# Layer 1 pipeline of a fused two-layer decoder: another order of the slots on TensorE and ScalarE

## What is computed

```python
# Lightning attention, 16 heads of 32, one chunk of 128 tokens
v, q, k = x @ Wv, x @ Wq, x @ Wk ; q, k = rotary(q), rotary(k)
o = (decay_mask * (q @ k.T)) @ v                    # per head
x = layernorm(x + (o * rsqrt(mean(o**2) + 1e-5) * rms_w) @ Wo)
# cross attention with ctx as keys and values: 8 heads of 16 tokens each,
# the 512 features are the positions
qk = einsum('hdq,hdl->hql', x_heads, ctx_heads) / sqrt(16)      # 512 x 512 per head
p = softmax(qk, axis=-1)
ret = einsum('hql,hdl->hdq', p, ctx_heads)
x = layernorm(x + gamma * ret)
```

## Time and profile before

| | |
|---|---|
| median of 3 runs | 3030.43 us (3025.59 to 3036.5) |
| the profiled execution | 3040.62 us |
| its span, first to last instruction | 3038.8 us |
| layer 0 | 0 to about 1164 us |
| layer 1 | about 1164 to 2061 us |
| experts | from about 2064 us |
| PE busy over the span | 2715.9 us (89%) |
| DVE / ACT / POOL busy | 45% / 29% / 19% |
| mean granted TensorE clock | 0.948 of 2.4 GHz |

### The profile page before, as it was taken

The page is one execution under the profiler, slowest core; times in us unless marked ns, Lnnn a source line. Parts: engine busy times, 40 slices in busy tenths (PEclk is TensorE's granted clock), DMA queues, the critical chain, the costliest instruction groups (busy, mean ns, idle before and its releaser), DMA issues. The chain is left out here.

```text
span 3038.8 us, 33792 instructions
## 1 busy us (share of the span) xinstructions
PE 2715.9 (89%) x10930; PEld 1371.9 (45%) x10990; DVE 1377.1 (45%) x2541; ACT 887.1 (29%) x1932; POOL 591.6 (19%) x632
## 2 busy tenths in 40 slices
PE   7999999999999765788888888867989999999998
PEld 3544553555455342333333333315445656656543
DVE  3545645564466253556566656642312222222245
ACT  2334343333434331134344434451001111111101
POOL 2111101110110001322222222200541111111153
PEclk9999999999999877999999999996999999999999
DMA  5110212021102104424444434323013333333144
GB/s 183 56 70 28 82 44 109 30 84 70 56 28 70 42 1 135 77 59 88 90 90 92 95 87 93 81 62 156 1 65 121 124 124 123 125 121 124 62 137 150
DMA packets 110237, 261.01 MB, mean 86 GB/s; under 512 B 21955, under 2 KB 55619, under 8 KB 98211
## 3 DMA queue, kind: packets, MB, share of 16 engines
q1 hardware_dynamic: 95202, 220.27, 24.3%
q0 software_dynamic: 13648, 38.06, 4.2%
q10 hardware_dynamic: 1264, 1.10, 0.1%
HBM read 203.76 MB, written 55.22 MB: 85 GB/s over the span
## 5 line engine op out<-in xcount | busy, mean ns | idle before, releaser
L2388 PE MATMUL d_bank<-d_w,d_xcol 128*128 x1280 | 406.4, 460 | 0.0
L1663 ACT ACTIVATE c_probs<-c_exp 128x512 f32<-128x512 f32 x512 | 277.9, 596 | 395.8 <-PE c_exp L1826 298.1
L1951 DVE TENSOR_REDUCE c_mx<-c_pair 128x2 f32<-128x1024 f32 x256 | 304.9, 1217 | 177.5 <-PE c_pair L1812 176.9
L742 PE MATMUL a_bank<-a_xT,a_ring 128*128 128x512 f32 x640 | 286.8, 600 | 10.9 <-DMA a_ident<-in_ident 10.9
L507 POOL TENSOR_TENSOR a_ry<-a_rt 128x512 f32<-128x512 f32 x80 | 128.8, 1610 | 803.0 <-DVE a_rt L994 803.0
L2388 PEld LDWEIGHTS d_bank<-d_w,d_xcol 128*128 128x128 f32 x1280 | 231.4, 191 | 102.1 <-issue 1.0
L2395 PE MATMUL d_bank<-d_w,d_hid 128*128 (+1 forms) x486 | 221.9, 592 | 0.7 <-DVE d_hid L2589 0.7
L742 PE MATMUL a_bank<-a_wo,a_ot 128*128 128x512 f32 x512 | 222.4, 592 | 0.0
L742 PEld LDWEIGHTS a_bank<-a_xT,a_ring 128*128 128x128 f32 x640 | 120.6, 192 | 150.0 <-issue 137.0
L1826 PE MATMUL c_exp<-c_qs,c_ks 128*128 128x512 bf16 x453 | 152.0, 392 | 35.4 <-ACT c_probs L1663 21.1
L2329 PE MATMUL d_bank<-d_xT,d_ws 128*128 128x512 f32 (+1 forms) x384 | 169.1, 601 | 0.7 <-ACT d_yrow L2309 0.7
(11 more groups left out here) (306 smaller groups left out, 3775.2 us busy)
## 6 DMA issues: line engine op xcount, KB each, us to landing
d_w<-in_w SPq DMA_DIRECT2D x16, 1408.0 KB, 6.5
scratch_results<-d_yrow SPq DMA_DIRECT2D x81, 256.0 KB, 2.0
a_ring<-in_wq SPq DMA_DIRECT2D x16, 1024.0 KB, 4.9
a_wo<-in_wo SPq DMA_DIRECT2D x16, 1024.0 KB, 4.9
c_ks<-scratch_kpark SPq DMA_DIRECT2D x96, 128.0 KB, 4.3
c_qs<-scratch_qpark SPq DMA_DIRECT2D x96, 128.0 KB, 4.3
d_w<-in_w SPq DMA_DIRECT2D x16, 768.0 KB, 8.4
a_ring<-in_w SPq DMA_DIRECT2D x8, 1024.0 KB, 8.4
```

Source lines behind the costliest of these rows:

```text
L742: ins = pe.matmul(bank[:, :], lhs(c), rhs(c), start=(c == 0), stop=(c == n - 1))
L1663: act.activation(probs[:, (LC * CH * n + k) % RING, :], bank[:, :], ACT.Exp, scale=float(CD) ** -0.5).then_inc(exped.sem, 1)
L1951: dve.tensor_reduce(mx[:, n % 2, at0:at0 + 2], bank[:, :].rearrange("p (i n) -> p i n", i=2), AX.X, ALU.max).then_inc(maxed.sem, 1)
L2388: ins = pe.matmul(bank[:, 0:FI], xcol[:, v, k, :], w13[:, bass.ds(at, 1), which, k, :].rearrange("p a n -> p (a n)"), start=(k == 0), stop ...
```

## The change

- `values` moves from the odd slots to the even ones, one slot earlier for each group of four exponentials (`turn_of`).
- `turn_x` moves from slot 0 of the phase in which its sequence is `a1` to slot 14 of the phase before (`TURN_X = 14`, for the new stage `a0 = p + 4`), between `scores` and `attend`; `PHASES` starts at -4. Its order in the small bank changes accordingly, and ACT copies it out in slot 15.
- `MAX_SLOTS` is 11: the 16 first products lie in 11 slots, and `TURN_MAX` is slot 11. DVE's `finish` and second `normalise`, and ACT's second root, come one slot earlier.
- In a slot ACT first drains the small bank (square, xT, sums, rms, v, turned q and k) and then does the two exponentials; the two roots of the layer norms stay behind the exponentials.
- The bank of the sum of squares counts as drained after the first of the two ACT steps of `rms_of`, which reads it, not after the second.
- On SP two rows of x are loaded ahead of the weights; after that `load_x(p + 5)` stands at the very end of a phase, behind `store(done)`, and from `p = 1` on it waits until that store has landed (`load_x` waits on `stored`).

```diff
-        rms_ready, y_added = signal("rms_ready", 1), signal("y_added", 1)
+        rms_step, y_added = signal("rms_step", 2), signal("y_added", 1)
-        PHASES = range(-3, SEQS + 1)
+        PHASES = range(-4, SEQS + 1)
         def stages(p):
-            return seq_at(p), seq_at(p + 1), seq_at(p + 2), seq_at(p + 3), seq_at(p - 1)
-        MAX_SLOTS = 12
-        TURN_X, SQUARES, OUT, V, Q, K = 0, 1, 2, 4, 6, 8
-        TURN_Q, TURN_K, TURN_MAX, SCORES, ATTEND = 10, 11, 12, 13, 15
+            return seq_at(p), seq_at(p + 1), seq_at(p + 2), seq_at(p + 3), seq_at(p + 4), seq_at(p - 1)
+        MAX_SLOTS = 11
+        SQUARES, OUT, V, Q, K = 1, 2, 4, 6, 8
+        TURN_Q, TURN_K, TURN_MAX, SCORES, TURN_X, ATTEND = 10, 11, 11, 13, 14, 15
         def turn_of(p, i):
-            if i % 2 == 0:
+            if i % 2:
                 return None
-            n, m = (p, (i - 3) // 2) if i >= 3 else (p - 1, TURNS - 1)
+            n, m = (p, i // 2 - 1) if i else (p - 1, TURNS - 1)
...
-                "ss": lambda: at(rms_ready, 1),
+                "ss": lambda: at(rms_step, 1),
...
             load_x(0)
+            load_x(1)
...
-                if seq_at(p + 4) is not None:
-                    load_x(p + 4)
                 if p > -2 and seq_at(p + 3) is not None:
                     load_c(p + 3)
                     load_cT(p + 3)
...
                 if done is not None:
                     store(done)
+                if p > -4 and seq_at(p + 5) is not None:
+                    load_x(p + 5)
...
             for p in PHASES:                       # scalar
                 for i in range(SLOTS):
-                    if x2 is not None:
-                        exp_of(x2, 2 * i)
-                        exp_of(x2, 2 * i + 1)
-                    if a2 is not None and i == TURN_X:
+                    if a2 is not None and i == 0:
                         square(a2)
-                    if a1 is not None and i == TURN_X + 1:
-                        turn_in(a1)
+                    if a0 is not None and i == TURN_X + 1:
+                        turn_in(a0)
...
                         turn(a1, 1)
-                    if done is not None and i == TURN_MAX + 2:
+                    if x2 is not None:
+                        exp_of(x2, 2 * i)
+                        exp_of(x2, 2 * i + 1)
+                    if a2 is not None and i == OUT + 2:
+                        root(a2, 0)
+                    if done is not None and i == SCORES:
                         root(done, 1)
...
             for p in PHASES:                       # tensor
                     if a1 is not None:
-                        if i == TURN_X:
-                            turn_x(a1)
...
                             attend(a1)
+                    if a0 is not None and i == TURN_X:
+                        turn_x(a0)
```

More of the change, by code:

```diff
@@ L1413, in build_layer1 @@
         for p in PHASES:
-            x2, x1, a2, a1, done = stages(p)
+            x2, x1, a2, a1, a0, done = stages(p)
             for i in range(SLOTS):
@@ L1424, in build_layer1 @@
                 if a1 is not None:
-                    for kind, at in (("xt", TURN_X), ("v", V), ("q", Q), ("k", K), ("qt", TURN_Q), ("kt", TURN_K),
-                                     ("a", ATTEND)):
+                    for kind, at in (("v", V), ("q", Q), ("k", K), ("qt", TURN_Q), ("kt", TURN_K), ("a", ATTEND)):
                         step_order += [(kind, a1)] if i == at else []
                     pair_order += [("s", a1, u) for u in range(2) if i == SCORES]
+                if a0 is not None:
+                    step_order += [("xt", a0)] if i == TURN_X else []
                 if (p, i) == FIX_TURN:
@@ L1682, in rms_of @@
                 bank = steps.wait(act, 0, ("ss", n))
-                astep.did(act.activation(lnv[:, 2:3], bank[:, 0:1], ACT.Ln, bias=eps[:, 0:1], scale=1.0 / D))
-                astep.wait(act, 0)
-                act.activation(rms[:, :], lnv[:, 2:3], ACT.Exp, scale=-0.5).then_inc(rms_ready.sem, 1)
+                act.activation(lnv[:, 2:3], bank[:, 0:1], ACT.Ln, bias=eps[:, 0:1], scale=1.0 / D)\
+                   .then_inc(rms_step.sem, 1)
+                rms_step.wait(act, n, 1)
+                act.activation(rms[:, :], lnv[:, 2:3], ACT.Exp, scale=-0.5).then_inc(rms_step.sem, 1)
             def root(n, i):
@@ L1715, in _ @@
                         rms_of(a2)
-                    if a2 is not None and i == OUT + 2:
-                        root(a2, 0)
                     if a1 is not None and i == V + 2:
@@ L1919, in add_y @@
                 bank = steps.wait(dve, 0, ("y", n))
-                rms_ready.wait(dve, n, 1)
+                rms_step.wait(dve, n, 2)
                 dve.scalar_tensor_tensor(row, bank[:, :], rms[:, 0:1], row, ALU.mult, ALU.add).then_inc(y_added.sem, 1)
@@ L1998, in _ @@
                         invert(done)
-                    if done is not None and i == TURN_MAX + 1:
+                    if done is not None and i == SCORES - 1:
                         finish(done)
@@ L2002, in _ @@
                         mask(a1)
-                    if done is not None and i == TURN_MAX + 3:
+                    if done is not None and i == SCORES + 1:
                         normalise(done, 1)
```

## The result

| | before | after |
|---|---|---|
| median | 3031.62 us (4 runs, 3025.59 to 3036.5) | 2913.68 us (4 runs, 2911.68 to 2917.99) |
| ratio | | 0.9614, 95% interval 0.9592 to 0.9635 |
| profiled execution | 3040.62 us | 2915.41 us |

The change gains 117.9 us, 3.9%. The forecast was 88 and its range ended at 2925, so it was too low by 30 us and the time lies outside the range.

The account below looks back on a forecast made before the run. PE was taken as the bound, its waits adding to each phase: 50.8 to 44.2 us saves 6.6, times 13 = 86, plus 2 at start and end = 88, giving 2943 us; range 2925 to 2987 at 0.8.

Parts of the forecast that it names:

- So 49.45 - 5.95 - 0.74 = 42.8 us of a phase is work: Clean phase of 49.45 us on PE, less 5.95 printed and 0.74 hidden waits, leaves 42.8 the change neither adds nor removes.
- The prediction's list of waits: PE's nine waits per clean phase: Wo, q, k, turned q, turned k, three at second products, turn_x; sum 5.95 us.
- Waits to come: New or remaining PE waits per phase: turned k 0.30, pairs of slots 12 and 13 0.35 and 0.1, attend 0.51; sum 1.4.
- The clock: First half of the Wo product, slow in 8 of 13 phases: full clock should hold with less waiting; otherwise 14 us less gain.
- Fits by 1 to 2 us: SP's chain from inverse to maxima takes 18.7 us plus c's loads, with 21.9 available: cost 0, else up to 2 per phase.
- Start and end: Load of x costs 1 us, phase -2 gains 2, phase -1 about 1, phases 13 to 16 nothing: together 2 us gained.
- The rivals: Four other outcomes: clock keeps falling (2956, 0.19), transfers bound (2975, 0.13), waits traded (3007, 0.10), slower at low clock (3048, 0.05).
- That of the transfers: Chain from inverse to maxima takes 2 to 3 us more, so slot 0 waits for DMA every phase: 2975 us, chance 0.13.
- that of the clock: Clock goes on falling because the stretch of turnings, scores and attend stays: 2956 us, chance 0.19.

Follow-up runs that it names:

- The forced waits: Changed kernel with PE waiting, in slots 3, 5 and 7 ahead of the second half product, on the slot's second exponential: 2993.27 us, ratio 0.9728.

## Why the prediction was too low, by its own steps

**The step that failed** is "So 49.45 - 5.95 - 0.74 = 42.8 us of a phase is work". It takes the idle time printed ahead of an instruction for the price of the wait, and the printed waits for all of them. The phases as measured leave 42.44 - 0.85 = 41.6 us of work, 1.2 less. The stretch from the first Wo half to turned q shows the error, since it holds the same instructions in both kernels: eight halves, eight pairs of second products, 22 matmuls of first products, four groups of values. Before it takes 1578.17 - 1548.34 = 29.83 us, after 1518.41 - (1534.12 - 42.44) = 26.73. The difference is 3.10, but only 0.74 + 0.67 + 0.67 = 2.08 was printed as idle. The timeline of PE before, at v, q and k:

```profile
1554.77 0.60 PE L1812 MATMUL c_pair<-c_ks,c_qs 96*128 96x512 bf16 x2
1555.44 1.96 PE L1784 MATMUL c_step<-c_wv,c_xT 128*128 128x512 f32 x4
...
1561.44 1.03 PE L1812 MATMUL c_pair<-c_ks,c_qs 96*128 96x512 bf16 x4
1563.20 1.95 PE L1784 MATMUL c_step<-c_wq,c_xT 128*128 128x512 f32 x4 [0.74 <-ACT c_v L1695]
1564.99 0.59 PE L1826 MATMUL c_exp<-c_qs,c_ks 128*128 128x512 bf16 x2
...
1569.20 0.60 PE L1812 MATMUL c_pair<-c_ks,c_qs 96*128 96x512 bf16 x2
1570.47 1.96 PE L1784 MATMUL c_step<-c_wk,c_xT 128*128 128x512 f32 x4 [0.67 <-DVE c_r L1944]
```

The idle time is counted from the modelled end of the group ahead, as 1561.44 + 1.03. Where nothing waits, the next group starts ahead of that end: the k half at 1514.74 stands 0.17 before 1514.31 + 0.60. So starts have to be compared with starts. The k half before starts 1570.47 - 1569.20 = 1.27 behind the first product, the one without a wait 0.43 behind it: it is 0.84 late, and 0.67 is printed. Three things make up the 1.02 us:

- Each of the three printed waits delays the start by about 0.17 more than is printed: 0.5.
- The first half of v starts 0.67 behind the first product and not 0.43: it is 0.24 late, and no wait is printed at all. The prediction's list of waits does not have it.
- The four first halves behind a wait (Wo, v, q, k) take 1.79 from start to start (1563.20 to 1564.99), where a half behind a first product takes 1.72 without a wait (1514.74 to 1516.46): 0.3.

By the Trainium skill, "TensorE: Matmul & The Clock Gate", "Step-by-step: what each phase is for", the drain of one matmul overlaps the next one's fill, and by its "Single matmul latency" the drain takes roughly 175 ns. The 0.17 us here are close to that, but they hang on the modelled ends and do not test it.

A wait thus cost 0.17 + 0.07 = 0.24 us on top of its printed idle time. The forced waits measured 0.27 each: the half starts 1.19 behind the first product for 0.43, with 0.58 printed, and takes 1.82 for 1.72.

In the other stretch, from turned q to the next Wo half, the sum of idle times was right: it fell by 1597.78 - 1578.17 - 15.71 = 3.90 us, and the idle time, shown and hidden, by 4.61 - 0.85 = 3.76. The 0.14 between them is about what the Wo product is late beyond its printed 1.06. So waits among the small matmuls cost hardly more than shown here. The other runs bear on it and do not settle it: with the exponentials first, 3.55 us more were printed and the phase grew by 3.67; with waits forced in slots 13 to 2, some 4.2 more were printed and the phases at full clock grew by 4.61.

**Waits to come: 1.4 forecast, 0.85 measured** (0.24 turned k, 0.30 attend, 0.31 inside the pair of slot 12). The places were right, and the pair of slot 13 hides its wait. So the clean phase: 49.45 forecast to 44.2, measured 42.44, the missing 1.76 being 1.02 from the first stretch (the price of waits and the unlisted one of v), 0.14 from the other stretch, 0.55 from new waits, and rounding. Over 13 phases that is 23 us.

**Which edit gives what** was partly wrong. The prediction gave turn_x 1.53 us and the shift of slots nothing. The steady phases in order of build-up are 49.44, 44.61 with values and drains, 42.93 with the shift, 42.44 with turn_x moved. Most of turn_x's wait goes with the drains, since the square then comes ahead of two exponentials; what is then late is DVE's maximum and mask, and these the shift brings forward.

**The clock: right.** All Wo halves take 1.88 to 1.99 in the inner phases, and the drains alone bring that on the kernel before. What the prediction drew from the Trainium skill, "TensorE: Matmul & The Clock Gate", part 4, that a third group of transposes ahead of attend would keep the clock falling, did not happen: the group is there, and the clock of the ten phases is 1.00. No run varies the transposes alone. Waits of some 4.7 us, most of them in slots 13 to 2, bring the falls back, as the forced ones show; whether as many elsewhere would, was not tried.

**SP: right, as a near thing.** "Fits by 1 to 2 us" became 0.3 us of waiting for the maxima per phase. The chain bounds nothing, and the load of x out of its middle helps: 2 us over the layer in the changed kernel (whose three profiles, the one with the late release of the bank among them, lie within 0.8), and with turn_x still in slot 0 about 0.5 per phase (566.47 against 559.62 over thirteen). The store lands in 3.8 us where the prediction took 2.3; behind it nothing is in a hurry.

**Start and end: 2 forecast, 8 to 11 measured** (the second profile of the kernel before has 118.74 and 1092.47 for the two stretches). Of the start's 5.35, phase -2 gives 35.84 - 33.27 = 2.6 and phase -1 1.2; the weights' first product comes 1.2 later; the remaining 2.8 are mostly shorter small products at a higher clock (scores 1.17 for 2.09, attend 1.08 for 1.94); why the clock was higher there stays open. At the end phase 13 shortens from 43.11 to 37.62: its Wo half was one of the slow ones (3.75, now 1.99), and a wait of 2.03 for DVE's maximum is gone (two later ones, 0.34 before, come to 1.17). The forecast counted 13 phases with the gain and left phase 13 out.

**The rivals.** None took place. That of the transfers came nearest, with 0.3 us per phase left on the queue; that of the clock is excluded by the windows.

## What to carry to other kernels

Price a wait ahead of a large product at its printed idle time plus what the stream loses by breaking, 0.24 to 0.27 us here, and look for late starts that print no wait; better, compare two stretches with the same instructions, one with the wait and one without. When several waits hang on one late engine, put its short drains ahead of its long work first and look again, because the other edits are then worth something else than their old waits say. Give the last, special phase its own line in the sum.

## What the runs showed of the hardware

- The granted clock fell without a long gap: in the kernel with waits in slots 13 to 2 no wait of the inner phases is longer than 1.3 us, and the clock was at 0.64 in the 4.7 us after them, while three waits of 0.58 us between weight products left it at 1.00.
- The same transfers land sooner or later by the order of the queue: the parked queries in 7.5 us with results ahead of them and in 2.3 when they go first; the maxima in 5.0 and 2.2, and in 1.9 in the kernel before.
- Two chips of the four take about 45 us longer, and in the kernels profiled there what follows phase 13 is longer by as much. Layer 1 shows no such difference: phases of 42.44 us stand in profiles of a slower chip (load of x in the middle) and of a faster one. No single kernel was profiled on both kinds.
